# Batches and experts stand one after another in the program instead of in loops on the engines

## The reference, cut to what matters

```python
x = x + xattn(layernorm(x), ctx_1024, Wq, Wk, Wv, Wo)       # 8 batches, 128 queries, 2048 context rows, 16 heads of 32
x = x + attn(layernorm(x), key, value, in_w, in_b, out_w, out_b)   # 8-bit fake quantisation, sequence axis 8
x = x + ffn(layernorm(x), router_w, w1, w2)                 # 8 experts, 2 of 8 per token, capacity 321

# xattn, per batch
Q, K, V = query @ Wq.T, context @ Wk.T, context @ Wv.T
out = softmax(Q K^T / sqrt(32)) V @ Wo.T
# ffn, per expert e over its at most 321 tokens
h = silu(buf[e] @ w1[e]); out_buf[e] = h @ w2[e]            # 512 -> 2048 -> 512
```

## Time and profile before

| | |
|---|---|
| median of 3 runs | 1791.84 us (1789.86 to 1792.25) |
| the profiled execution, its own time | 1790.3 us |
| its span, first to last instruction | 1788.8 us |
| PE busy | 1638.2 us, 92% |
| DVE, ACT, POOL busy | 1195.1, 746.7, 488.1 us |
| mean granted TensorE clock | 0.958 |

### The profile page before, as it was taken

One profiled execution on the slowest core, in us unless ns is written; L12 is line 12 of the kernel. 1 busy time (PEld: TensorE's weight loads), 2 busy tenths in 40 slices (PEclk: granted clock), 3 DMA queues, 4 the chain that ended last, 5 costly groups with the idle time before them and its releaser, 6 DMA issues. The chain is left out here.

```text
span 1788.8 us, 42535 instructions
## 1 busy us (share of the span) xinstructions
PE 1638.2 (92%) x17518; PEld 1121.5 (63%) x17518; DVE 1195.1 (67%) x1380; ACT 746.7 (42%) x932; POOL 488.1 (27%) x421
## 2 busy tenths in 40 slices
PE   6899899999999999999999999694658999999996
PEld 4656566666666666666666666473435777777774
DVE  5668467567658657657657656376787776666765
ACT  5335235444445444444444344205443444444441
POOL 2323232232132132122123146333056411001133
PEclk9999999999999999999999999696879999999998
DMA  6524343234234234234234233440037565555543
GB/s 244 143 65 113 72 107 96 46 98 104 46 89 113 46 87 115 46 84 119 46 84 114 50 76 100 148 164 2 2 131 247 164 199 185 190 173 193 175 130 110
DMA packets 101984, 201.79 MB, mean 113 GB/s; under 512 B 25724, under 2 KB 25724, under 8 KB 101707
## 3 DMA queue, kind: packets, MB, share of 16 engines
q1 hardware_dynamic: 91114, 169.49, 33.0%
q0 software_dynamic: 10720, 30.02, 6.3%
HBM read 127.36 MB, written 18.90 MB: 82 GB/s over the span
## 5 line engine op out<-in xcount | busy, mean ns | idle before, releaser
L566 DVE TENSOR_REDUCE mx<-sc 128x4 f32<-128x2048 f32 x128 | 293.3, 2291 | 89.3 <-PE sc L788 88.7
L427 ACT ACTIVATE probs<-sc 128x1024 f32<-128x1024 f32 x256 | 248.2, 1024 | 72.2 <-PE sc L821 71.4
L390 ACT ACTIVATE v_sb<-proj 128x512 f32<-128x512 f32 x128 | 76.4, 597 | 368.6 <-PE proj L749 368.6
L329 POOL TENSOR_TENSOR acc_g<-probs 128x1024 f32<-128x1024 f32 x31 | 73.1, 2359 | 512.8 <-ACT probs L427 512.7
L588 DVE TENSOR_TENSOR acc_v<-acc_v,probs 128x1024 f32<-128x1024 f32 x93 | 129.5, 1393 | 88.1 <-ACT probs L427 85.5
L749 PE MATMUL proj<-w_hi,ctx_hi 128*128 128x256 f16 x1024 | 161.4, 282 | 15.8 <-ACT ctx_hi L379 12.4
L1040 DVE SCALAR_TENSOR_TENSOR w_lo<-stage_w,w_hi 128x2048 f16<-128x2048 f32 x64 | 144.6, 2289 | 34.6 <-ACT w_hi L1034 33.6
L749 PE MATMUL proj<-w_lo,ctx_hi 128*128 128x256 f16 x1024 | 160.2, 281 | 1.2 <-DVE w_lo L522 1.2
L749 PE MATMUL proj<-w_hi,ctx_lo 128*128 128x256 f16 x1024 | 159.7, 280 | 0.2 <-DVE ctx_lo L528 0.2
L534 DVE SCALAR_TENSOR_TENSOR k_lo<-proj,k_hi 128x512 f16<-128x512 f32 x128 | 87.9, 687 | 106.7 <-ACT k_hi L399 105.9
L2091 PE MATMUL po<-h_hi,w_lo 128*128 128x321 f16 x496 | 149.2, 301 | 1.1 <-issue 1.1
(11 more groups left out here) (336 smaller groups left out, 2828.1 us busy)
## 6 DMA issues: line engine op xcount, KB each, us to landing
stage_w<-in_w SPq DMA_DIRECT2D x64, 1024.0 KB, 5.8
stage<-in_ctxT SPq DMA_DIRECT2D x64, 512.0 KB, 6.9
ks<-k_hi SPq DMA_DIRECT2D x256, 128.0 KB, 2.4
ks<-k_lo SPq DMA_DIRECT2D x128, 128.0 KB, 2.4
wq_f<-in_wiT POOLq DMA_DIRECT2D x24, 256.0 KB, 4.3
xg<-xbuf POOLq DMA_DIRECT2D x28, 176.0 KB, 4.0
obuf<-o_sb POOLq DMA_DIRECT2D x28, 176.0 KB
xbuf<-final SPq DMA_DIRECT2D x17, 256.0 KB
```

The source lines that it names most:

```text
L390: act.activation(v_sb[:, half, 2 * n:2 * n + 2, :], proj[where % 2][:, :].rearrange("p (c d) -> p c d", c=2), ACT.Copy, scale=1.0 / WSCALE ...
L427: act.activation(probs[:, u % 4, :], unit_scores(u), ACT.Exp, scale=1.0 / sqrt(HD)).then_inc(e_ready, 1)
L566: dve.tensor_reduce(mx[:, :, kb], sc[:, :, :], AX.X, ALU.max).then_inc(m_read, 1)
```

## The change

Each of the ten loops becomes a Python loop at build time. The bodies stand six times (seven for SP's experts) one behind the other with constants in the waits and addresses. Nothing else is edited, and the order of what computes or moves data is the same on each engine.

```diff
@@ cross-attention, SP @@
                 body(0, False)
-                with nc.Fori(1, B - 1, engines=(mybir.EngineType.SP,), hint_back_edge=True) as b:
+                for b in range(1, B - 1):
                     body(b, False)
                 body(B - 1, True)
@@ cross-attention, DVE @@
-                with nc.Fori(1, B - 1, engines=(mybir.EngineType.DVE,), hint_back_edge=True) as b:
+                for b in range(1, B - 1):
                     loop_steps = Steps(dve, v_step, FIRST_STEPS + PER * (b - 1))
                     body(b, False, loop_steps)
@@ cross-attention, PE (POOL and ACT in the same way) @@
-                with nc.Fori(1, B - 1, engines=(mybir.EngineType.PE,), hint_back_edge=True) as b:
+                for b in range(1, B - 1):
                     body(b, False)
                 body(B - 1, True)
...
@@ experts, SP @@
-                with nc.Fori(1, E_, engines=(mybir.EngineType.SP,), hint_back_edge=True) as e:
+                for e in range(1, E_):
                     for s in range(8):
                         load(e, s)
@@ experts, PE (POOL, ACT and DVE in the same way) @@
-                with nc.Fori(1, E_ - 1, engines=(mybir.EngineType.PE,), hint_back_edge=True) as e:
+                for e in range(1, E_ - 1):
                     body(e, False)
                 body(E_ - 1, True)
```

More of the change, by code:

```diff
@@ L360, in _ @@
                 load_weight(1, 1)
-                with nc.Fori(1, B - 1, engines=(mybir.EngineType.Pool,), hint_back_edge=True) as b:
+                for b in range(1, B - 1):
                     body(b, False)
@@ L511, in _ @@
                 body(0, False)
-                with nc.Fori(1, B - 1, engines=(mybir.EngineType.Activation,), hint_back_edge=True) as b:
+                for b in range(1, B - 1):
                     body(b, False)
@@ L1789, in _ @@
                     gp.dma_start(whose[0:ROWS[i], i, :], last_rows[P * i:P * i + ROWS[i], :]).then_inc(whose_in, 16)
-                with nc.Fori(1, E_ - 1, engines=(mybir.EngineType.Pool,), hint_back_edge=True) as e:
+                for e in range(1, E_ - 1):
                     body(e)
@@ L1862, in _ @@
                 body(0, False)
-                with nc.Fori(1, E_ - 1, engines=(mybir.EngineType.Activation,), hint_back_edge=True) as e:
+                for e in range(1, E_ - 1):
                     body(e, False)
@@ L2047, in _ @@
                 body(0, False)
-                with nc.Fori(1, E_ - 1, engines=(mybir.EngineType.DVE,), hint_back_edge=True) as e:
+                for e in range(1, E_ - 1):
                     body(e, False)
```

## The result

The kernel after takes 1780.71 us (median of 5 runs, 1777.85 to 1783.56) against 1790.06 us for the kernel before in the same rounds (1788.06 to 1792.25). The ratio is 0.9947, with an interval of 0.9931 to 0.9964: 9.35 us or 0.5% faster. The prediction was 1789.7 us, in a range from 1785.0 to 1793.5 us. The one stretch that it named behaves as it said; the rest of the gain comes from places where it expected nothing or nearly nothing.

The account below looks back on a forecast made before the run. PE's own products were taken to bound the loops. -1.9 us behind the cross-attention's loop and -0.2 us for branches made -2.1 us, 1790.3 to 1788.2 us profiled, so 1789.7 us as median; range 1785.0 to 1793.5 us.

Parts of the forecast that it names:

- The one stretch that it named: g0 of batch 7, first after PE's cross-attention loop: 40.80 us, expected about 38.8, or 37.2 if the clock holds.
- the stall: PE idle 3.35 us without a releaser at the start of batch 7, read as code not there yet.
- The code behind the loop: Start of batch 7: stall goes, a 2.3 us wait for DVE's maximum replaces it, round 1 moves forward 3.56 us.
- The clock behind that wait: Batch 7's g0: half clock follows the new wait as in five of six g3, costing 1.64 us; 1.9 us gained.
- Branches and register work: All loops: PE has instructions queued over its back edges, other engines' work is covered by PE's products; -0.2 us.
- the 2.03 us waits in g3 should be there still: Sign in the profile after: PE's waits for DVE in g3 of the looped batches stay at 2.03 us.
- The back edges: PE's branches between looped batches of the cross-attention: 0.2 us in sum, nothing in the experts.
- By it the 1.64 us are due: Clock rule from the skill page: a wait inside a tight stream makes work behind it start cold, costing 1.64 us.
- Experts at nothing: Experts' loop: PE has no gap before, in or behind it, so nothing to gain; six stay at 317.6 us.
- Code transfers at nothing: Instruction fetches of all engines: counted 0, bounds -0.2 us to 3.35 us for each packet that comes late.
- late code on another engine: Rival: ACT and DVE fetch every batch anew, late packets delay PE; 18 us slower, 1807.7 us; chance 0.10.
- nothing takes the stall's place: Rival at batch 7's start: DVE's maximum comes earlier or the clock holds; up to 5.9 + 0.2 us, 1785.7 us; chance 0.22.

Follow-up runs that it names:

- e3: Kernel before with only PE's loop of the cross-attention unrolled, the other nine loops kept: 1784.90 us, ratio 0.9978.
- e4: Kernel before with all loops unrolled but PE's of the cross-attention: 1784.53 us, ratio 0.9974.
- e5: Kernel before without the prefetch hint for the back edge of PE's cross-attention loop: 1807.61 us, ratio 1.0096.
- e2: The changed kernel once more, nothing edited: 1780.51 us, ratio to before 0.9954.
- e7: Changed kernel with DVE making g3's first maximum before g2's last sum, in every batch but the last: 1764.82 us, ratio to before 0.9864.
- e11: Changed kernel with the first of four transposes of a batch done four times, to restore the old batch length: 1784.78 us, ratio to before 0.9990.
- e14: Changed kernel with two one-column fills on DVE ahead of the maximum of g3: 1782.53 us, ratio to before 0.9972.
- e12: Changed kernel with e7's edit, also for g2 of batch 0, and the weights' maxima moved behind batch 1's first group's maxima: 1755.06 us, ratio to before 0.9822.
- e15: Changed kernel with eight one-column fills on DVE ahead of the maximum of g3: 1783.81 us, ratio to before 0.9983.
- e1: The kernel before once more, against itself, nothing edited: 1790.03 us, ratio 1.0001.
- e8: Kernel before with only the five loops of the experts unrolled: 1788.31 us, ratio 0.9996.
- e10: Kernel before with only POOL's loop of the cross-attention unrolled, executed once for its profile: waits in g3 of 1.94 to 1.95 us.

## Why the prediction was right about the stall and wrong about the size

**The code behind the loop: right, in place and size.** The stall was late code (e3, e4, e5), it went, and the wait for DVE's maximum is 2.26 us where 2.3 was forecast. The Trainium skill, page "Runtime: NRT & Kernel Launch", section "Instruction fetch mechanics", prefers unrolled kernels because a taken branch to code that isn't held forces a fetch. Here that holds for the taken branches without the hint (3.4 to 3.8 us each, e5); with it, the price stood at the branch that wasn't taken.

**The clock behind that wait: the other outcome came.** The sum took 1.64 us; in after, e2, e3, e5, e7, e11 and e14 the clock held, with g0 at 37.2 us, and only e12 and e15 lost it. The step from 40.79, 39.19 and 38.93 us (before, e1, e8) to 37.2 is worth 2.4 us on the mean, and 1.9 us over all eight profiles in which PE's loop stands, against the 1.9 us of the sum. That the size came out is partly luck: the working rested on the first profile of before, whose stall of 3.35 us, as large as in e10 and larger than in the six others (2.64 to 2.93 us), made up for the clock that was put too low.

**Branches and register work: the step that failed.** It said that "their covers are PE's products, on which all of them wait", and counted -0.2 us for PE's back edges and nothing for the other engines. That is true where DVE has slack. In the last part of g2 it has none: ACT's and POOL's work leads into a DVE with no pause over about 0.1 us, whose last instruction is the maximum that PE waits for in g3. There 0.08 us of ACT and 0.08 us of POOL lie on the path, 0.16 us in each of six batches, 1.0 us. The bound ("at most some 0.1 us per wait") was too low for this wait and was put into the range rather than the sum, though the earlier trace rows showed that PE waits for this very chain. The expectation that "the 2.03 us waits in g3 should be there still" fell by the same step: they are there, at 1.87 us.

**The back edges: mis-sized, in the same step.** The waits view shows 0.2 us once. From the start of a batch's last product to the first of the next, PE takes 0.35 to 0.47 us over the branch (before, e1, e8) and 0.20 us in after, so that each of the five back edges costs 0.15 to 0.27 us, 1.0 us together. The view lists only the longest of such short gaps, and the groups of the earlier trace rows begin behind the boundary. The earlier trace rows had the time: in g3 of batch 3 PE is idle for 2.17 us (36.80 less 34.63), of which the wait takes 2.03; in after the idle time of g3 is the wait alone (36.40 less 34.52, 1.88 us).

**What hangs on the shorter batches.** The prediction kept the half clocks of the looped g3 at their number, five of six in its one profile, and so put them at nothing in the sum. They are 4.7 of six in the mean of before, e1 and e8, and three in after and in e2: 1.7 × 1.64 = 2.8 us, the largest part of what was missed. By the reading above the reason is the place of the waits in time; how much of it belongs to the wait and how much to the back edge can't be told apart. That it is no accident of these profiles is supported by all executions: on the chip of e1 and e2 the mean granted clock was 0.9584 before (25 executions) and 0.9603 after (6), an estimate of 3 to 4 us less lost to the clock in the whole kernel. The Trainium skill, page "TensorE: Matmul & The Clock Gate", section "HAM oscillation — how this bites in real kernels", tells that a wait in a tight stream can make the work behind it start cold. Its example is a wait of 3 to 5 us, so the prediction's "By it the 1.64 us are due" took more from it than it states; behind the waits of about 2 us here it came in 48 of 84 cases.

**The account.** Behind the loop 1.9 to 2.4 us, back edges 1.0, waits in g3 1.0, half clocks 2.8: about 7 of some 9 us. The other two or so are not placed, and the spread from run to run is of their size.

**The other steps.** Experts at nothing: right (317.60 us; e8). Code transfers at nothing: right (15 more packets for PE in the experts, 18 for 3, where "some 20 more" were named, and no gap). Of the rivals, late code on another engine didn't come, and "nothing takes the stall's place" came nearest in time, 1785.7 us, but the gain came by another way than it told.

## What to carry to other kernels

Where an engine waits at the end of a chain over several engines, price every instruction in the chain by that wait, register work in front of the releasers included, and look at what follows the wait. Here batches shorter by 0.31 us met the half clock in three of six cases instead of 4.7, which was worth more than the time taken out; such a gain hangs on where the waits fall in time and need not come in another kernel. And before unrolling for such a wait, ask whether the order on the busy engine lets it vanish: one maximum moved ahead of one sum gained over twice as much as ten unrolled loops.

## What the runs showed of the hardware that was not expected

- PE's loop with the hinted back edge paid at its exit, 2.64 to 3.35 us, and only 0.15 to 0.27 us at each back edge; without the hint it paid 3.4 to 3.8 us at every back edge and nothing at its exit.
- A register instruction between a wait and the work behind it cost 0.08 us on POOL (0.16 us from the releaser's end to the start instead of 0.08), and 0.08 us on ACT's chain; on DVE nothing showed.
- Whether a wait of 1.86 to 2.04 us was followed by half clock, at 1.64 us each, hung on the place of the wait against the moments at which the clock can change (46 of 48 waits that began 0.0 to 1.2 us behind one, 2 of 36 elsewhere), and on its length only at the edge; with waits of 2.02 to 2.03 us it was 22 of 30 cases in five profiles and 1 of 6 in e5.
- Fills of one column on DVE, 0.06 us each in the trace, lengthened PE's wait by 0.01 to 0.02 us each (e14, e15), where I had reckoned with 0.05 to 0.1 us.
